# A decoder block: cross-attention in two passes with keys on partitions, and expert weights spread by DMA and multiplied in by GpSimd

## The chip, the cores and the metric

The kernel runs on one core of a Trainium2 chip. The core has five engines that run side by side and wait for each other by semaphores: TensorE (PE, matrix multiplications into PSUM), VectorE (DVE), ScalarE (ACT), GpSimd (POOL) and SyncE (SP, which here only issues DMAs). The metric is the time of one execution on the device in microseconds; the lower the better.

## The reference: what is computed

A block of a decoder over 128 sequences of 64 tokens with 128 features each. Three stages follow each other, each with a layer norm ahead and a residual behind:

```
x = x + attention(norm(x))          # 16 heads of 64, through 8 pooled "agent" queries per head
x = x + cross_attention(norm(x), ctx, ctx)   # 16 heads of 8, causal mask, softmax over 64 keys
x = x + ffn(norm(x))                # 16 experts of 64, each token takes 2; and one shared layer

scores  = Q K^T / sqrt(8) + causal                 # cross-attention, per sequence and head
out     = (softmax(scores) V) Wo^T
combine = one_hot(top 2 of 16 by a gate) * gate weight      # ffn, 16 numbers a token
h       = silu(x We1 + be1) * (x We3 + be3)                 # all experts for all tokens
y       = sum over e of combine[e] * (h[e] We2[e] + be2[e])
```

## The kernel before

The 128 sequences are taken in 8 groups of 16, 1024 tokens each. Each engine has its own program, written out by hand, and all five follow the same plan, `both(e, g)`: the feed-forward of group e is interleaved with the two attentions of group e + 1 = g. Nothing reorders it later: an engine that waits holds all that stands behind it in its own program. `both(None, 0)` opens, seven calls of `both(e, e + 1)` follow, `both(7, None)` closes.

The feed-forward goes in 18 units k = 0 to 17: two chunks of 512 tokens, in each one shared layer and then eight pairs of experts, with the hidden features of a pair on 128 partitions and tokens along the free dimension. A unit is `up(e, k)`, two groups of three fp32r matmuls over 512 tokens (rows L491 to L493) into the banks H1 and H3; SiLU of H1 by ACT into `sil` (L874); for a pair a bf16 matmul `weight`, named C, that spreads the combine weights over the partitions (L500); two passes of DVE, `hidden_3` (L1166) and `weighted` (L1173), which make `hT`; and `down_to(e, k)`, four fp32 matmuls that add hT times w2 to Y (L510). `unit(e, k)` issues `up(k)`, C, and `down_to(k - 1)`. The C matmul needs the combine weights with experts on partitions: DVE's `gate` makes them, split into three bf16 parts, and PE transposes them.

The cross-attention goes in four rounds u of four sequences. `scores` puts queries on partitions and heads and keys along the free dimension, in four banks S (L598 the mask, L606 the scores, on tiles of 32 rows and 64 columns). DVE takes the maximum over keys (`maxima`, L1219, L1221) and subtracts it (L1222), ACT takes the exponential into `pr` (L930, L935), DVE sums and inverts (`inverses`, L1233, L1235), POOL normalises 14 of the 16 blocks (L426) and DVE two. Then PE transposes the probabilities (`turn`, L624), ACT copies them (`PT_moved`), and PE multiplies with the values (`values`, L635) and projects (`project`, L648). `add_x` (L1239) adds the residual; a layer norm (`norm`, POOL's power, `apply`, L1080) gives xn3, the input of the feed-forward.

The first attention begins with `moments`, 8 blocks M_0 to M_7 of four fp32 matmuls (L674) on pooled sums (L1286), then `scores_1` (L541) and `scores_2` (L552), `soften` on DVE (subtracting maxima, L1187 to L1193), exponentials on ACT, `normalise_2` on DVE (three passes, L1200 to L1202), transposes of the probabilities p1T and p2T, `pool_tokens` (L581) and three more blocks. In the feed-forward of the same call these stand between the units; `gate_shift` and `gate` (L1088 to L1144) are DVE's part of the choice of experts, from the gate matmul (L720) on.

Where the rows name a tile as `PXUT`, `KQ` or `M`, it is the buffer in which the tile of that moment lies; several share one.

Of the kernel before, what the change touches and what calls it, by code (L numbers as in the profile page):

```python
# [6 lines left out]
def decoder_block(nc, x, ctx_in, Wqkv, Wo_a, bo, Wq, Wk, Wv, Wo_x, gate_w, gate_b,  # L7
# [16 lines left out]
    B, S, D = x.shape  # L24
    P = 128
# [12 lines left out]
    BY_DVE = (XQ * UX - 4, XQ * UX - 3)  # L38
    BY_POOL = [k for k in range(XQ * UX) if k not in BY_DVE]
# [3 lines left out]
    CHUNKS = TOK // CH  # L43
    EPS = 1e-5
# [12 lines left out]
    att = ["ctxT_0", "ctxT_1", "V_0", "V_1", "V_2", "xnT1_0", "xnT1_1", "V_3", "KT_0"]  # L57
    att += [f"M_{n}" for n in range(8)]
    att += ["s1_0", "s1_1", "s2_0", "KT_1", "s1_2", "s1_3", "s2_1"]
    att += ["p1T_0", "p2T_0", "PX_0", "PX_1", "p1T_1", "p2T_1", "PX_2", "PX_3"]  # L60
    att += [f"UT_{n}" for n in range(4)] + [f"U_{n}" for n in range(4)] + ["Ya_0", "Ya_1"]
    att += ["xnT2_0", "xnT2_1", "QT_0", "QT_1"] + [f"S_{n}" for n in range(XQ * UX)]
# [4 lines left out]
             "h1": (["xnT3_0"] + [f"H1_{k}" for k in range(UNITS)], 1),  # L67
             "h3": (["xnT3_1"] + [f"H3_{k}" for k in range(UNITS)], 1),
             "c": (["gate", "combS"] + [f"C_{k}" for k in PAIRED if k < EP + 1] + ["combT_0", "combT_1"]
                   + [f"C_{k}" for k in PAIRED if k > EP], 1),  # L70
             "y": (["Y_0", "Y_1"], 1),

             "pt": ([f"PT_{n}" for n in range(2 * T)], 2),
             "ol": ([f"OL_{u}" for u in range(UX)], 1),
# [7 lines left out]
    with ExitStack() as ctx:  # L82
# [9 lines left out]
        Kx, Qx = KQ[:, 0:4, :], KQ[:, 4, :]  # L92
# [14 lines left out]
        woM = sb("woM", [P, 2, 2, D])  # L107
# [13 lines left out]
        identb = sb("identb", [P, P], bf16)  # L121
        maskb = sb("maskb", [P, 2, HALF, S], bf16)
        pick = sb("pick", [P, 2, S], bf16)
        planes = sb("planes", [P, 4, 4])
        plane = sb("plane", [P, 4])
        onehot3 = sb("onehot3", [P, E], bf16)
        spread = sb("spread", [P, EP, 2, EI], bf16)
# [11 lines left out]
        xnT3 = sb("xnT3", [P, TOK])  # L139
# [27 lines left out]
        Vb = sb("Vb", [P, T, XH // 2, 2, 2 * XC])  # L167
        mx = sb("mx", [P, XQ, HALF])
        lx = sb("lx", [P, 2, XQ, HALF])
        rx = sb("rx", [P, 2, XQ, HALF])  # L170

        PR = 3 * XQ
        pr_a = PXUT[:].rearrange("p a b h -> p (a b h)").rearrange("p (k h s) -> p k h s", k=2 * XQ, s=S)
# [16 lines left out]
        comb = sb("comb", [P, T, 2 * E])  # L190
        combs = sb("combs", [P, T, P], bf16)
        combT = sb("combT", [P, TOK])
        combsT = sb("combsT", [P, TOK], bf16)
        sil = sb("sil", [P, 2, CH])
        hT = sb("hT", [P, 2, CH])

# [1177 lines left out]
```

## Time and profile before

| what | us |
|---|---|
| median of 3 runs (1148.31 to 1152.15) | 1151.69 |
| the profiled execution: span from first to last instruction | 1150.6 |
| PE busy in it | 975.8 (85%) |
| DVE busy | 788.8 (69%) |
| ACT busy | 577.3 (50%) |
| POOL busy | 227.7 (20%) |

The share of busy time says little by itself: two stretches alternate eight times, one filled by PE, and one in which the engines wait for each other in turn. The chain of waits tells them apart, as does the busy time by window. In rows of the timeline, a group of instructions stands with its start, its length, the engine, the line, what it writes from what, and how many records it has; fp32 matmuls leave two records each. In brackets stands the idle time before it and who ended it. The granted clock of PE is given as a share of 2.4 GHz, so 0.50 is 1.2 GHz.

### The profile page before, as it was taken

Reading aid. Unit: us, or ns where it says so; the run is one execution under the profiler, and the core shown is the slowest. Engines: PE = TensorE matmul, PEld = TensorE weight load, DVE = VectorE, ACT = ScalarE, POOL = GpSimd, SP = SyncE. Lnnn points to the kernel's source line nnn. Section 1 sums busy time; section 2 is a strip of 40 time slices with the busy share of each in tenths; the row PEclk is TensorE's granted clock in tenths of the full one; section 3 lists DMA queues with packets and bytes.
Section 4 is the critical chain, followed back from the end, with each engine's and each line's share of the span. In section 5 each row is a group of like instructions: output and inputs, shape, how many; then the busy total and the mean of one; then the engine's idle time right before and its main releaser. Section 6 shows DMA issues by size and latency. Waiting matters only on the chain.

```text
span 1150.6 us, 22137 instructions
## 1 busy us (share of the span) xinstructions
PE 975.8 (85%) x9069; PEld 767.2 (67%) x9069; DVE 788.8 (69%) x1841; ACT 577.3 (50%) x1148; POOL 227.7 (20%) x220
## 2 busy tenths in 40 slices
PE   6656899969998799978999699987999689987687
PEld 5553688737785587846886487855787477864566
DVE  3256866687866967678667878678666867669444
ACT  4434755367534665357553565346652575445322
POOL 6001410035000520024100440014200341004100
PEclk9886999979998899979999799989999799997789
DMA  5300010000100010000100010000100000000000
GB/s 146 80 1 1 2 38 1 11 10 2 38 10 10 2 38 1 11 10 2 37 11 1 11 31 8 10 11 2 38 1 10 11 2 1 10 11 1 1 1 19
DMA packets 28902, 18.36 MB, mean 16 GB/s; under 512 B 7649, under 2 KB 27394, under 8 KB 28802
## 3 DMA queue, kind: packets, MB, share of 16 engines
q1 hardware_dynamic: 26914, 12.48, 4.2%
q0 software_dynamic: 1280, 4.20, 1.2%
q8 instruction: 72, 1.18, 0.4%
q10 hardware_dynamic: 608, 0.27, 0.1%
q14 instruction: 28, 0.23, 0.1%
HBM read 12.62 MB, written 4.19 MB: 15 GB/s over the span
## 4 chain that ended last, share of the span: by engine, by line
PE 62%; DVE 21%; ACT 10%; POOL 3%; issue 3%; SPq 1%; DMA 0%; DVEq 0%; POOLq 0%
PE banks L510 7%; PE banks L674 5%; PE banks L491 5%; PE banks L493 5%; PE banks L492 5%; PE banks L606 4%; PE banks L624 4%; ACT M L867 3%; PE banks L648 3%; DVE PXUT L1222 3%; DVE mx L1221 3%; PE banks L769 3%; PE banks L541 2%; DVE sil L1166 2%; PE banks L598 2%
## 5 line engine op out<-in xcount | busy, mean ns | idle before, releaser
L874 ACT ACTIVATE sil<-banks,b 128x512 f32<-128x512 f32 x144 | 99.5, 691 | 199.6 <-PE banks L493 197.2
L867 ACT COPY M<-banks 128x512 f32<-128x512 f32 x208 | 122.9, 609 | 90.3 <-PE banks L624 70.2
L1166 DVE SCALAR_TENSOR_TENSOR sil<-banks,b,sil 128x512 f32<-128x512 f32 x128 | 95.8, 749 | 93.6 <-ACT sil L874 91.8
L510 PEld LDWEIGHTS banks<-w,hT 128*128 128x128 f32 x1152 | 151.5, 194 | 12.5 <-issue 7.2
L510 PE MATMUL banks<-w,hT 128*128 128x128 f32 x1152 | 154.5, 277 | 1.4 <-DVE hT L1173 1.4
L389 POOL DMA_DIRECT2D out_x<-xn x16 | 12.9, 809 | 534.3 <-DVE xn L1179 534.3
L426 POOL TENSOR_TENSOR PXUT<-PXUT,rx 128x512 f32<-128x512 f32 x80 | 87.2, 1117 | 101.7 <-DVE rx L1235 101.7
L1173 DVE TENSOR_TENSOR hT<-sil,banks 128x512 f32<-128x512 f32 x128 | 87.9, 687 | 25.1 <-PE banks L500 21.3
L624 PE MATMUL banks<-ident,PXUT 128*128 128x128 f32 x384 | 61.9, 301 | 31.7 <-ACT M L867 28.2
L598 PE MATMUL banks<-maskb,pick 32*64 32x512 bf16 x512 | 46.4, 506 | 46.6 <-ACT PXUT L930 28.2
L674 PEld LDWEIGHTS banks<-pooled,A 128*128 128x128 f32 x512 | 66.1, 207 | 19.9 <-DVE pooled L1286 18.6
L624 PEld LDWEIGHTS banks<-ident,PXUT 128*128 128x128 f32 x384 | 44.1, 150 | 52.6 <-ACT M L867 40.0
L674 PE MATMUL banks<-pooled,A 128*128 128x128 f32 x512 | 68.9, 293 | 12.0 <-DVE pooled L1286 12.0
L491 PE MATMUL banks<-xnT3l,w1h 128*128 128x512 f32 x144 | 75.1, 522 | 0.3 <-ACT sil L874 0.3
L491 PE MATMUL banks<-xnT3l,w3h 128*128 128x512 f32 x144 | 61.4, 427 | 11.1 <-DVE sil L1166 10.3
L1221 DVE TENSOR_REDUCE mx<-banks 128x8 f32<-128x512 f32 x96 | 65.3, 681 | 0.0
L867 ACT COPY PXUT<-banks 128x512 f32<-128x512 f32 x64 | 36.0, 588 | 54.6 <-PE banks L581 30.7
L606 PE MATMUL banks<-KQ 32*64 32x256 f32 x1024 | 60.9, 547 | 0.0
L493 PE MATMUL banks<-xnT3h,w1h 128*128 128x512 f32 x144 | 59.3, 412 | 0.0
L493 PE MATMUL banks<-xnT3h,w3h 128*128 128x512 f32 x144 | 59.2, 411 | 0.0
L1233 DVE TENSOR_REDUCE lx<-PXUT 128x8 f32<-128x512 f32 x96 | 59.2, 658 | 0.0
L492 PE MATMUL banks<-xnT3h,w1l 128*128 128x512 f32 x144 | 59.2, 411 | 0.0
(199 smaller groups left out, 2067.2 us busy)
## 6 DMA issues: line engine op xcount, KB each, us to landing
xin<-in_x SPq DMA_DIRECT2D x8, 512.0 KB, 4.1
cin<-in_ctx SPq DMA_DIRECT2D x8, 512.0 KB, 5.3
out_x<-xn POOLq DMA_DIRECT2D x16, 256.0 KB, 2.8
KQ<-in_L_attn_Wqkv SPq DMA_DIRECT2D x3, 512.0 KB, 5.3
KQ<-in_L_ffn_We SPq DMA_DIRECT2D x2, 512.0 KB, 4.6
KQ<-in_L_attn_Wo SPq DMA_DIRECT2D x1, 512.0 KB, 8.0
w<-in_L_ffn_We SPq DMA_DIRECT2D x1, 512.0 KB
woM<-xwT SPq DMA_DIRECT2D x16, 8.0 KB, 1.8
```

What stands on the lines that cost most here:

```text
L491: mm(ps(name)[:], wh[:, 2 * p:2 * p + 2, :], xl, start=True, stop=False)
L492: mm(ps(name)[:], wl[:, 2 * p:2 * p + 2, :], xh, start=False, stop=False)
L493: mm(ps(name)[:], wh[:, 2 * p:2 * p + 2, :], xh, start=False, stop=True).then_inc(fulled(name), 1)
L510: mm(ps(name)[:, P * t:P * t + P], hT[:, k % 2, P * t:P * t + P], w2[:, pair[k], :], start=(n == 0 and t == 0), stop=False, skip_group_che ...
L606: last = mm(ps(name)[64 * r:64 * r + 64, 256 * t:256 * t + 256], Qx[rr, S * b:S * b + S], Kx[rr, :, S * b:S * b + S], start=False, stop=Tr ...
L624: last = turn_over(ps(name)[:, P * j:P * j + P], src[:, P * j:P * j + P], ident[:])
L674: last = mm(ps(f"M_{n}")[:, P * k:P * k + P], A[:, 4 * (n % 4) + k, :], pooled[:], start=True, stop=True)
L867: cp(dst, ps(name)[:] if src is None else src).then_inc(ready, 1)
L874: nc.scalar.activation(sil[:, k % 2, :], ps(f"H1_{k}")[:], ACT.Silu, bias=b1[:, pair[k]:pair[k] + 1]).then_inc(sil_ready, 1)
L1166: V.scalar_tensor_tensor(sil[:, k % 2, :], ps(f"H3_{k}")[:], b3[:, p:p + 1], sil[:, k % 2, :], ALU.add, ALU.mult).then_inc(hid_ready, 1)
L1173: V.tensor_tensor(hT[:, k % 2, :], sil[:, k % 2, :], ps(f"C_{k}")[:], ALU.mult).then_inc(hT_ready, 1)
L1221: link(V.tensor_reduce(mx[:, q], sv, AX, ALU.max), g)
```

## The change

The cross-attention is done in two passes. The first keeps the scores with queries on partitions, but only their maxima are taken. These, one per query and head, are split in three bf16 parts and transposed into `shiftT` (`split_shifts`, `turn_shifts`). In the second pass `scores_T` computes the scores again with keys on partitions, with the mask and the negated maximum added by a bf16 matmul (`pickT` and `shiftT`), so that ACT takes the exponential straight from PSUM and the probabilities need no transpose. The values carry a column of ones (`Vx`), so that `values` gives the sums too, and `normalise_O` divides the 8 columns of a head by the ninth. `turn_O`, a copy and `project` follow.

The combine weights are transposed in fp32, written to DRAM (`comb_d`) and read back by two DMAs a unit, each spreading one expert's row over 64 partitions, into a ring of four (`cw`). POOL multiplies them into `sil` (`weight` of POOL), and `hidden` is one pass of DVE. `down_to` runs two units behind `up` (`LAG`), H3 has two banks.

The order changes too. The rounds of first-pass scores stand between units 13 to 16, and the transposes and moments of the next group stand in the second pass. The core of the diff:

```
-    att = ["ctxT_0", "ctxT_1", "V_0", "V_1", "V_2", "xnT1_0", "xnT1_1", "V_3", "KT_0"]
-    att += [f"M_{n}" for n in range(8)]
+    front = ["ctxT_0", "ctxT_1", "xnT1_0", "xnT1_1"] + [f"M_{n}" for n in range(8)]
...
+             "h1": (["xnT3_0", "H1_0", "H1_1", "combT_0", "combT_1"] + [f"H1_{k}" for k in range(2, UNITS)], 1),
+             "h3": (["xnT3_1"] + [f"H3_{k}" for k in range(UNITS)], 2),
+             "f": (front, 2),
...
+            def weights_spread(e):
+
+                sp.wait_ge(combT_ready, 2 * e + 2)
+                sp.dma_start(comb_d.ap(), combT[0:E, :]).then_inc(comb_stored, 16)
+                sp.wait_ge(comb_stored, 16 * e + 16)
+                for n, k in enumerate(PAIRED):
+                    use = len(PAIRED) * e + n
+                    c, p = k // (EP + 1), pair[k]
+                    if use >= CW:
+                        sp.wait_ge(weighted, use - CW + 1)
+                    for a in range(2):
+                        row = comb_d.ap()[2 * p + a, CH * c:CH * c + CH]
+                        sp.dma_start(cw[EI * a:EI * a + EI, use % CW, :],
+                                     row.partition_broadcast(EI)).then_inc(cw_loaded[use % CW], 16)
...
+            def weight(e, k):
+
+                if e is None or k not in PAIRED:
+                    return
+                use = len(PAIRED) * e + PAIRED.index(k)
+                pool.wait_ge(cw_loaded[use % CW], 32 * (use // CW) + 32)
+                pool.wait_ge(sil_ready, UNITS * e + k + 1)
+                s = sil[:, k % (LAG + 1), :]
+                nc.gpsimd.tensor_tensor(s, s, cw[:, use % CW, :], ALU.mult).then_inc(weighted, 1)
...
+            def scores_T(g, u):
+
+                names = [f"ST_{XQ * u + q}" for q in range(XQ)]
+                if u == 0:
+                    pe.wait_ge(mT_ready, g + 1)
+                for q, name in enumerate(names):
                     wait_free(pe, g, name)
...
+                    for j in range(2):
+                        mm(ps(name)[:, 256 * j:256 * j + 256], pickT[:, 2 * q + j, :, :],
+                           shiftT[:, 256 * u:256 * u + 256], start=(j == 0), stop=False, skip_group_check=True)
+                for j in range(2):
+                    for k in range(4):
+                        b = 4 * u + k
+                        for q, name in enumerate(names):
+                            rr = slice(32 * q, 32 * q + 32)
+                            c0 = 256 * j + S * k
+                            last = mm(ps(name)[:, c0:c0 + S], Kx[rr, j, b, :],
+                                      Qx[rr, S * b:S * b + S], start=False, stop=True, skip_group_check=True,
+                                      tile_position=(32 * q, 0))
...
+                pe.wait_ge(ex_ready, XS * g + XQ * u + XQ)
+                for t in range(2):
+                    for j in range(XH // 2):
+                        for r in range(2):
+                            k = 2 * t + r
+                            c0, w = 256 * (j % 2) + S * k, 2 * (XC + 1)
+                            o0 = w * (XH // 2) * t + w * j
+                            last = mm(ps(name)[64 * r:64 * r + 64, o0:o0 + w],
+                                      PT[:, XQ * (u % 2) + j // 2, c0:c0 + S], Vx[:, 4 * u + k, j, :],
+                                      start=True, stop=True)
...
+                wait_full(act, g, f"ST_{k}")
+                nc.scalar.activation(PT[:, k % (2 * XQ), :], ps(f"ST_{k}")[:], ACT.Exp).then_inc(ex_ready, 1)
...
+                wait_full(dve, e, f"H3_{k}")
+                if k in PAIRED:
+                    dve.wait_ge(weighted, len(PAIRED) * e + PAIRED.index(k) + 1)
...
+                p, slot = pair[k], k % (LAG + 1)
+                V.scalar_tensor_tensor(hT[:, slot, :], ps(f"H3_{k}")[:], b3[:, p:p + 1], sil[:, slot, :],
+                                       ALU.add, ALU.mult).then_inc(hT_ready, 1)
```

Three places where the programs' order changes. The first is PE's program from the last values of a group to the gate matmul of its feed-forward, before (L635 are the values, L648 the projection, L674 the moments, L720 the gate):

```order
L635 MATMUL banks<-M,Vb 32x128 x16
L660 MATMUL banks<-xwT,ctxT 64x64 x8
L648 MATMUL banks<-woM,KQ 64x128 x8
L469 MATMUL banks<-ident,xn 128x128 x8
L660 MATMUL banks<-xwT,ctxT 64x64 x8
L666 MATMUL banks<-ctxT,xwT 128x512
L674 MATMUL banks<-pooled,A 128x128 x16
L469 MATMUL banks<-ident,xn 128x128 x8
L674 MATMUL banks<-pooled,A 128x128 x4
L720 MATMUL banks<-gwT,xnT 128x16 x8
```

And after the change (L658 are the values, L667 `turn_O`, L676 the projection, L546 and L557 `scores_1` and `scores_2`, L745 the gate):

```order
L658 MATMUL banks<-Vx,PXUT 64x18 x32
L667 MATMUL banks<-ident,KQ 128x128 x2
L676 MATMUL banks<-xwT,KQ 128x128 x2
L688 MATMUL banks<-xwT,ctxT 64x64 x32
L488 MATMUL banks<-ident,xn 128x128 x8
L546 MATMUL banks<-xnT,M 128x128 x8
L557 MATMUL banks<-M,xnT 64x128 x8
L745 MATMUL banks<-gwT,KQ 128x16 x8
```

The moments and the first transposes (L469 with 8 matmuls ahead of L660) no longer stand between the projection and the gate; the values of the next group's keys (L688) do, and the first score blocks stand ahead of the gate.

The second is DVE's program where the combine weights are done, after the change (L1145 is the last pass of `gate`, L1186 to L1188 are `normalise_2`, L1158 is `hidden`):

```order
L1145 TENSOR_TENSOR comb<-gate 128x8x16
L1186 TENSOR_REDUCE l<-PXUT 128x64
L1187 RECIPROCAL r<-l 128x64
L1188 TENSOR_TENSOR PXUT<-PXUT,r 128x512
L1158 SCALAR_TENSOR_TENSOR hT<-banks,b,sil 128x512
L1186 TENSOR_REDUCE l<-PXUT 128x64
L1187 RECIPROCAL r<-l 128x64
L1188 TENSOR_TENSOR PXUT<-PXUT,r 128x512
L1158 SCALAR_TENSOR_TENSOR hT<-banks,b,sil 128x512
```

The L1158 in the middle is `hidden` of unit 1, the first that needs combine weights. Before, the two `normalise_2` stood after the hidden passes of units 4 and 5.

The third is PE's program in the second pass, after the change, from the first round's transposed scores (L633 mask and shift, L641 scores) to the third round's moments (L702):

```order
L633 MATMUL banks<-shiftT,pickT 128x256 x8
L641 MATMUL banks<-KQ 128x64 x32
L488 MATMUL banks<-ident,xn 128x128 x8
L658 MATMUL banks<-Vx,PXUT 64x18 x32
L633 MATMUL banks<-shiftT,pickT 128x256 x8
L641 MATMUL banks<-KQ 128x64 x32
L667 MATMUL banks<-ident,KQ 128x128 x2
L702 MATMUL banks<-pooled,A 128x128 x8
L676 MATMUL banks<-xwT,KQ 128x128 x2
L658 MATMUL banks<-Vx,PXUT 64x18 x32
```

Between the scores and the values of a round stands work of the next group, and the projection of the round before.

## Rows read from the trace of the kernel before

**Rows 1.** Chain of waits in order of time: start us, us, what.

```profile
43.02 1.14 DVE pooled L1286
...
142.29 1.14 DVE pooled L1286
...
940.58 1.14 DVE pooled L1286
```

**Rows 2.** Busy by window: window, us, PE, PEld, DVE, ACT, POOL (instructions), clock, DMA.

```profile
365.00:375.00 10.00, 5.37 (x73) 2.27 (x81) 7.87 (x14) 4.79 (x13) 0.79 (x1) 0.60 0.09 26
```

**Rows 3.** Groups by line: what, how many, busy us, mean ns, idle before.

```profile
L426 POOL TENSOR_TENSOR PXUT<-PXUT,rx 128x512 f32<-128x512 f32 x80 | 87.2, 1117 | 101.7 <-DVE rx L1235 101.7
```

**Rows 4.** Timeline of PE, feed-forward of group 1 to first scores: start us, us.

```profile
303.60 0.58 PE L491 MATMUL banks<-xnT3l,w1h 128*128 128x512 f32 x1
...
341.21 0.48 PE L491 MATMUL banks<-xnT3l,w1h 128*128 128x512 f32 x1
...
342.69 0.39 PE L500 MATMUL banks<-combsT,spread 128*128 128x512 bf16 x1
...
343.74 0.48 PE L491 MATMUL banks<-xnT3l,w1h 128*128 128x512 f32 x1
...
360.71 1.04 PE L606 MATMUL banks<-KQ 32*64 32x256 f32 x32
```

**Rows 5.** Timeline of PE, other small matmuls (weights rows*columns, then moving shape).

```profile
30.71 1.62 PE L660 MATMUL banks<-xwT,ctxT 128*64 128x64 f32 x48 [0.78 <-ACT ctxT L867]
...
276.52 3.84 PE L674 MATMUL banks<-pooled,A 128*128 128x128 f32 x32 [0.40 <-DVE pooled L1286]
...
282.50 1.96 PE L720 MATMUL banks<-gwT,xnT 128*128 128x16 f32 x16 [0.38 <-ACT xnT L867]
...
316.38 1.16 PE L581 MATMUL banks<-p1T,xn 64*128 64x128 f32 x16
```

**Rows 6.** Timeline of DVE: `apply` of xn3, and `add_x` one period on.

```profile
277.09 2.14 DVE L1080 TENSOR_SCALAR xn<-xe,norm_e 128x128 f32<-128x128 f32 x8 [0.62 <-POOL norm_e L397]
...
406.58 0.42 DVE L1239 TENSOR_TENSOR xe<-xr,banks 128x256 f32<-128x256 f32 x1 [0.24 <-PE banks L648]
```

**Rows 7.** Timeline of DVE: from `gate_shift` to the last pass of `gate`.

```profile
284.50 0.29 DVE L1088 TENSOR_REDUCE g<-banks 128x8 f32<-128x128 f32 x1 [5.27 <-PE banks L720]
...
293.56 0.75 DVE L1166 SCALAR_TENSOR_TENSOR sil<-banks,b,sil 128x512 f32<-128x512 f32 x1 [0.94 <-ACT sil L874]
...
297.22 0.29 DVE L1144 TENSOR_TENSOR combs<-gate,combs 128x128 bf16<-128x128 f32 x1
```

**Rows 8.** Timeline of DVE: `soften` and what follows it, `normalise_2` and what follows it.

```profile
297.43 0.42 DVE L1187 TENSOR_REDUCE m<-banks 128x4 f32<-128x256 f32 x1
...
300.34 0.68 DVE L1173 TENSOR_TENSOR hT<-sil,banks 128x512 f32<-128x512 f32 x1
...
314.89 0.68 DVE L1200 TENSOR_REDUCE l<-PXUT 128x64 f32<-128x512 f32 x1
...
316.80 0.74 DVE L1166 SCALAR_TENSOR_TENSOR sil<-banks,b,sil 128x512 f32<-128x512 f32 x1
```

**Rows 9.** Timeline of ACT: a copy of transposed combine weights, and its wait for PE.

```profile
330.35 0.57 ACT L867 COPY combT<-banks 32x512 f32<-32x512 f32 x1 [0.45 <-PE banks L477]
```

**Rows 10.** DMA issues: what, queue, how many, KB each, median us to landing.

```profile
xin<-in_x SPq DMA_DIRECT2D x8, 512.0 KB, 4.1
...
woM<-xwT SPq DMA_DIRECT2D x16, 8.0 KB, 1.8
```

**Rows 11.** Busy by window, columns as in rows 2: where the clock fell and rose.

```profile
366.00:367.00 1.00, 0.45 (x16) 0.35 (x24) 1.00 (x2) 0.47 (x1) 0.00 (x0) 0.96 0.00 0
...
377.00:378.00 1.00, 1.00 (x7) 0.60 (x5) 0.97 (x3) 0.53 (x2) 1.00 (x2) 0.92 0.00 0
```

**Rows 12.** Timeline of POOL at the start, and of PE at the last xn3.

```profile
18.54 0.66 POOL L380 TENSOR_SCALAR_AFFINE_SELECT maskb<-maskb 32x512 bf16<-32x512 bf16 x1
...
1078.29 1.97 PE L469 MATMUL banks<-ident,xn 128*128 128x128 f32 x8 [5.88 <-DVE xn L1080]
```

More of the change, by code:

```diff
@@ L37, in decoder_block @@
     UX = T // 2
-    BY_DVE = (XQ * UX - 4, XQ * UX - 3)
-    BY_POOL = [k for k in range(XQ * UX) if k not in BY_DVE]
+    XS = XQ * UX
     E, EG, EI = 16, 4, 64
@@ L268, in wait_free @@
             ring, k, use, _, at = place[name]
+            if not use and ring in ("o", "yx") and not g:
+                return
             if use:
@@ L962, in both @@
+            def both(e, g):
+                nxt = g + 1 if g is not None and g + 1 < GROUPS else None
+                if e is None:
+                    ctx_moved(g)
+                    xn_moved(g)
+                    for n in range(8):
+                        M_moved(g, n)
+                if g is not None:
                     for n in range(4):
-                        M_moved(g, n)
+                        V_moved(g, n)
                 if e is not None:
@@ new lines, in both @@
+                if g is not None:
+                    apply("a", xr, xn, rstd_ready, 2 * g + 2, xn_ready, lambda: hidden(e, 8))
+                else:
+                    hidden(e, 8)
+                for k in range(9, 11):
+                    hidden(e, k)
+                result(e, 0)
+                hidden(e, 11)
+                hidden(e, 12)
+                for u in range(UX):
+                    if g is not None:
+                        maxima(g, u)
+                    hidden(e, 13 + u)
@@ new lines, in both @@
+                if g is not None:
+                    split_shifts(g)
+                hidden(e, 17)
+                result(e, 1)
+                if g is None:
+                    return
+                if nxt is not None:
+                    dve.wait_ge(x_loaded, 16 * nxt + 16)
+                    norm(nxt, "a", xin, var_ready)
+                    apply("a", xin, xn, rstd_ready, 2 * nxt + 1, xn_ready)
+                for u in range(UX):
+                    normalise_O(g, u)
+                    if u == 0 and nxt is not None:
+                        dve.wait_ge(xnT_ready, 4 * nxt + 2)
+                        V.tensor_reduce(pooled[:], xnT[:, 0:TOK].rearrange("p (k s) -> p k s", s=S // POOL), AX,
+                                        ALU.add).then_inc(pooled_ready, 1)
+                    if u:
+                        add_x(g, u - 1)
+                        if u < UX - 1:
+                            stats_e(g, u - 1)
```

719 lines of the change are left out of this document (298 added, 421 removed).

## The prediction

> **What bounds the kernel now.** I read the busy times first (TensorE, PE, is busy 85% of the span, no other engine above 69%), then the chain of waits in order of time, then one period of the timeline engine by engine. The chain repeats: the pooled sums of group 1 start at 142.29 and those of group 7 at 940.58 [rows 1], so a group takes (940.58 - 142.29) / 6 = 133.05 us. In the feed-forward stretch PE is the bound: a unit of the hidden layer is `up` (six matmuls, 341.21 to 342.69), the combine-weight matmul C and `down` (to 343.74), and the next starts at once [rows 4]. In the cross-attention PE waits: from 365 to 375 it is busy 5.37 of 10 us at 0.60 of its clock while VectorE (DVE) is busy 7.87 [rows 2]. So two things can gain: PE's own units, and this second stretch.
>
> **The change part by part.** All times below run along one new period, from the moment T at which the normalised rows xn3 are ready to the next T. Prices are at the full granted clock first; the clock is a term of its own. A PE row's time runs some 0.1 us into the next row's; that is taken off.
>
> *Passes taken off.* Sixteen hT passes, twelve subtractions, sixteen sums and the normalising of the probabilities leave DVE and GpSimd (POOL). That is worth only what PE waited for them. On PE a unit loses C: 1.05 us for C and `down` together, of which C is a 512-column matmul like one of the six in `up`, 1.48 / 6 = 0.25; a unit goes from 2.53 to 2.29 [rows 4], 18 x 0.24 = 4.3 us per group. POOL's 16 new multiplications take the place of 14 old ones of the same shape, 1.12 us each [rows 3]; at one per 2.29 us unit, with `down` now two units behind, they are hidden.
>
> *1. From T to the combine weights: 18.7 us.* PE does the xn3 transposes (8 single passes, each half of a 276.52 matmul: 0.9), two score blocks (8 matmuls like those of the 276.52 row, 1.8, and half-width ones, 0.5) and the gate (1.81, the 282.50 row) [rows 5]: gate full at T+5.1. DVE is in soften(0) until then, does gate_shift (0.65) and then soften(1), which stands ahead of the gate now and takes 300.34 - 297.43 = 2.9 [rows 8]; its last input comes at T+7.4, so it ends at T+9.0. The chain in the old order ran from 284.50 to 297.51 = 13.0 [rows 7]. Off go gate_shift and its exponential (two passes of 0.29 and one of 0.3 on ScalarE, 1.0), the hidden pass that moves with its wait (0.94 + 0.75), and the splitting (four passes like the 297.22 row, 1.05); 9.3 remain, and 0.4 of waiting for the first SiLU, which queues behind soften(1)'s exp. T+18.7. PE has 12.2 us of work in that time (0.9 + 1.8 + 0.5 + 1.8 + 1.8 + 0.5, two `up` and the keys, 2.0); the moments that filled it are gone to the other end of the period. 6.4 us idle.
>
> *2. From there to the transpose p2T_1: 11.9 us.* The weights are transposed twice through one bank, 0.65 + 0.57 + 0.65 + 0.57 with the copies [rows 9] = 2.5; written to DRAM (2.3, between 1.8 for 8 KB and 4.1 for 512 KB [rows 10]); read back spread over 64 partitions, twice (2.4 by the same rows, and 0.45 for the second issue); multiplied by POOL (1.1) and DVE (0.75). Behind DVE's hidden(1), which waits for all this, is queued normalise_2(1) (316.80 - 314.89 = 1.9 [rows 8]), and PE's p2T_1 waits for that, with all units from 3 on behind it. Five semaphore hops, 0.5. PE has 6.6 us of work here, so 5.3 idle. Bounds: 10.8 with both transfers at 1.8, 15.5 with both at 4.1.
>
> *3. From p2T_1 to the end of the feed-forward: 57.6 us.* PE-bound as before. From unit 3 to the end of the first scores it took 303.60 to 361.75 = 58.15 [rows 4]. Off: 14 C (3.4), three of four transposes of the probabilities (1.4), one pooling block (1.1), two weight transposes (0.9), old waits (1.8). On: two `down` (1.6), the bias matmuls (0.9), three score rounds (3 x 1.45), new waits (1.2: each score round waits for four maxima). Each score round now hides behind a unit, which is the change's real gain: DVE needs 3.4 of the 3.8 us.
>
> *4. The second pass: 39.2 us.* Per round, eight bf16 matmuls of 256 columns (half of C, 0.12 each: 1.0), 32 of 64 columns on 32-row tiles, and 32 value matmuls of 18 columns. The trace has none of these two. In records of a weight load with its pass (two per fp32 matmul), the nearest rows: 32 records on 32-row tiles in 1.04 us, 33 ns [rows 4]; 16 on 64-row tiles in 1.16 (68 ns with the next start), 48 with 64-column weights in 1.62 (34 ns), 16 of 16 columns on the whole array in 1.81 (113 ns) [rows 5]. I take 33 ns x 64 = 2.1 for the transposed scores (1.0 if it goes by columns, 4.4 by the 68 ns) and 34 ns x 64 = 2.2 for the values (1.1; 3.6, half of 113 ns for half the weight columns). Four rounds of 5.3 = 21.2. Between scores and values PE waits for four exponentials (0.6 each, like the copy of [rows 9], a copy among them and hops: 3.0), which moments partly fill: round 0 waits for xn of the next group, ready 7.3 after the pass starts (3.3); round 1 3.0; rounds 2 and 3 hold three moments of 0.92 [rows 5] over two banks, whose third waits for a copy behind the exponentials (4.9 each). 16.1, and 1.85 for the shifts' transposes and copy: 39.2.
>
> The Trainium skill, "TensorE: Matmul & The Clock Gate", section "LDWEIGHTS (loading the stationary operand)", says that a load's time follows the weight's columns and not its depth. By its figure 128 columns are 107 ns (an estimate from that page of the Trainium skill), and a round's 64 loads one after the other 6.8 us instead of 2.1. The 16-record row on 64-row tiles [rows 5] speaks against that for tiles, with 68 ns for such a load.
>
> *5. From the last values to T: 8.7 us.* normalise_O (0.85), transpose, copy and projection (1.6), then the old chain from add_x to xn3: 406.58 less a period is 273.53, to 277.09 + 2.14 = 279.23: 5.7 [rows 6], plus 0.5 for two more statistics. PE has 3.0 of filler (values of the next group); 4.2 idle at a stretch.
>
> Sum: 18.7 + 11.9 + 57.6 + 39.2 + 8.7 = 136.1 us, against 133.05. The old waits of the cross-attention come back as three waits of DVE and DMA chains that no PE work covers.
>
> *6. The clock: +7 us per period.* In the old period the clock fell to 0.5 (1.2 GHz) at 366.9 after some 4 us in which PE did little, and rose at 377.2 [rows 11]: 10 us, which cost some 5. The measured 133.05 holds that already. The old tail shows PE idle 5.88 us behind the chain of part 5 [rows 12]. The new period has four such places: the idle of 5 (1.5), of 1 (0.5, hidden by 2), of 2 (2, on units that bound) and the sparse first rounds of 4 (3). These are estimates from that stretch; bounds 0 and 14.
>
> *7. Head, last group, tail.* First T before: 1078.29 - 7 x 133.05 = 146.9. GpSimd's five new masks of 64 x 1024 (at least 0.66 each [rows 12], 1.2 by size) and larger clears bring the constants 6.3 later, but the pooled sums no longer wait for the expert weights (43.02 [rows 1], now 36.7). The key copies on ScalarE give 5 of these back, 2.3 remain. From the first scores to T it was 279.23 + 133.05 - 360.71 = 51.6; now four rounds of 4.1 without units, the splitting (17.7), 38.4 and 8.7 = 64.8, and clock 3. Head +13.9. The last group has no moments: -5.5. Tail: 14 units x 0.24 less the longer start, -1.4.
>
> Total: 1150.6 + 13.9 + 7 x (136.1 + 7 - 133.05 = 10.05) - 5.5 - 1.4 = 1228; the profiled span is 1 us below the median, so **1229**.
>
> **The rivals.** *Full clock.* As above with 6 at nothing: 1150.6 + 10.9 + 7 x 3.05 - 6.9 = 1176. For it: PE's longest hole is 5.3. Against: it fell after less at 366.9 [rows 11]. *The other side: small matmuls go by their columns and the clock holds.* Then 4 is 4 x 2.2 = 8.8 shorter, the period 127.3: 1150.6 + 2.1 - 7 x 5.75 - 6.9 = 1106. It decides from a period of 133, that is, if 4 loses more than the 3 us by which the sum is over. *Loads one after the other*: by the 113 ns row a round is 7.2 instead of 2.1, 32 rounds x 5.1 = +163: 1392; the 68 ns row speaks against it. It is where the rule of the Trainium skill cited above would lead. *Transfers that set the pace* instead of only the start: a ring of four units (9.2 us) covers 4.1 + 0.9, so only 2 grows, by 8 x 3.6 at most: 1258, inside the range.
>
> **How the numbers follow.** Forecast with the clock's term 0.56, full clock 0.18, loads in series 0.04: slower 0.78. Columns and clock 0.18 faster; 0.04 lands within 0.3%, about what a measurement here can tell from no change. The prices' ends are -70 and +118, the clock's -50 and +50, seldom together: 1140 to 1300 leaves out most of the faster case (0.14) and the serial loads (0.04).
>
> **What would show it.** Right: PE idle some 6 us before the weight transposes and 5 before p2T_1, the latter released by DVE behind hidden(1); a period near 143; granted clock 0.5 after these. Wrong: value and score records far off 34 and 33 ns; PE idle under 2 us at either place; DVE or GpSimd as releaser in most units.

## The result, and the profile after

The changed kernel takes 1258.38 us (median of 4 runs, 1257.78 to 1260.06) against 1150.47 for the kernel before: a ratio of 1.094, 95% interval 1.092 to 1.096. Forecast were 1229 and slower; the range 1140 to 1300 holds the time. The medians and ratios below leave out one run as slow, 1200.47 us of the three edits together.

The chain of waits of the changed kernel, in order of time (start us, length us, what), shows the places T at which xn3 is ready, eight in all; it answers to [rows 1] and the `apply` of [rows 6]:

```profile
156.18 2.15 DVE xn L1088 x8
...
301.07 2.15 DVE xn L1088 x8
447.49 2.15 DVE xn L1088 x8
593.79 2.15 DVE xn L1088 x8
...
1034.17 2.15 DVE xn L1088 x8
1183.05 2.15 DVE xn L1088 x8
```

So the first T is at 158.3, the periods are 144.9, then five of 146.3 to 147.2, and the last 148.9. The period from T = 303.2 to 449.6 is the one that the parts below are read from. Its timeline of PE, from the first two `up` to unit 4 (L496 turns the combine weights over, L574 is p2T_1, L510 begins an `up`):

```profile
319.12 0.39 PE L512 MATMUL banks<-xnT3h,w3h 128*128 128x512 f32 x1
324.37 1.04 PE L496 MATMUL banks<-ident,comb 128*32 128x128 f32 x4 [4.86 <-DVE comb L1145]
...
333.03 0.66 PE L567 MATMUL banks<-ident,e 128*128 128x128 f32 x4
337.51 1.09 PE L574 MATMUL banks<-ident,PXUT 128*128 128x128 f32 x4 [3.83 <-DVE PXUT L1188]
338.25 0.78 PE L510 MATMUL banks<-xnT3l,w1h 128*128 128x512 f32 x1
...
343.03 0.50 PE L510 MATMUL banks<-xnT3l,w1h 128*128 128x512 f32 x1
```

PE's two longest waits here are 4.86 us before the weights' transposes and 3.83 before p2T_1; behind the second the `up` of unit 3 takes 0.78 where that of unit 4 takes 0.50. The granted clock by window (window, us, PE, PEld, DVE, ACT, POOL busy, clock, DMA share, GB/s) says why:

```profile
322.00:324.00 2.00, 0.00 (x0) 0.00 (x0) 1.78 (x7) 2.00 (x4) 0.00 (x0) 0.97 0.00 0
324.00:326.00 2.00, 1.04 (x4) 0.43 (x4) 1.91 (x4) 0.73 (x2) 0.00 (x0) 0.50 0.00 0
...
328.00:330.00 2.00, 2.00 (x8) 1.71 (x7) 0.00 (x0) 1.16 (x2) 0.00 (x0) 0.50 0.24 41
...
338.00:340.00 2.00, 2.00 (x7) 1.71 (x6) 1.71 (x5) 0.67 (x2) 0.00 (x0) 0.50 0.26 94
```

The second pass, same timeline (L633 the pick, L641 transposed scores, L658 values, L488 the next group's transposes):

```profile
400.73 2.01 PE L641 MATMUL banks<-KQ 32*128 32x64 f32 x64
405.24 1.49 PE L488 MATMUL banks<-ident,xn 128*128 128x128 f32 x8 [2.50 <-DVE xn L1088]
406.66 3.61 PE L658 MATMUL banks<-Vx,PXUT 128*64 128x18 f32 x64
410.20 1.89 PE L633 MATMUL banks<-shiftT,pickT 128*128 128x256 bf16 x8
412.02 3.69 PE L641 MATMUL banks<-KQ 32*128 32x64 f32 x64
...
420.03 2.05 PE L658 MATMUL banks<-Vx,PXUT 128*64 128x18 f32 x64
422.01 1.05 PE L633 MATMUL banks<-shiftT,pickT 128*128 128x256 bf16 x8
422.99 2.01 PE L641 MATMUL banks<-KQ 32*128 32x64 f32 x64
...
431.40 1.05 PE L633 MATMUL banks<-shiftT,pickT 128*128 128x256 bf16 x8
...
438.82 2.05 PE L658 MATMUL banks<-Vx,PXUT 128*64 128x18 f32 x64
```

PE waits 2.50 us for xn of the next group; from then to about 419 its clock is 0.50, and the same 64 records take 3.6 us instead of 2.0:

```profile
406.00:408.00 2.00, 2.00 (x30) 1.67 (x28) 0.00 (x0) 1.10 (x2) 0.00 (x0) 0.50 0.00 0
...
418.00:420.00 2.00, 2.00 (x13) 1.91 (x11) 0.00 (x0) 0.96 (x3) 0.00 (x0) 0.64 0.00 0
```

A round at full clock takes 9.39 (422.01 to 431.40). Spans and mean granted clock, of the kernel before and then of the changed one:

```profile
core 0: 1150.6 us, clock 0.921
```

```profile
core 0: 1256.3 us, clock 0.880
```

At two levels, 1.0 and 0.5, that is 2 x 0.079 x 1150.6 = 182 us at half clock before, and 2 x 0.120 x 1256.3 = 301 after: 120 us more, worth up to 60 of the 106 us wherever PE is the bound. Whole periods, columns as above: one before, then the one above and the last group's after the change:

```profile
279.23:412.28 133.05, 117.75 (x1126) 92.61 (x1125) 97.12 (x230) 70.72 (x143) 26.32 (x22) 0.94 0.05 13
```

```profile
303.22:449.64 146.42, 126.22 (x1420) 108.25 (x1420) 70.51 (x183) 54.59 (x96) 31.65 (x24) 0.90 0.14 41
...
1036.32:1185.20 148.88, 122.33 (x1276) 102.81 (x1276) 65.21 (x159) 44.97 (x76) 30.00 (x23) 0.80 0.11 33
```

Of the 13.4 us by which a period grew, PE is busy for 8.5 and waits for 4.9. By the same sum these periods hold some 16, 29 and 60 us at half clock, and the last one of the kernel before (944.40 to 1078.25, granted clock 0.91) 24, so the last group alone brings some 36 of the 120.

### The profile page after: what moved, and what is told of

The parts are those of the page before. It is cut to its first block, busy times and chain, and to the rows that moved or that the text cites. A ratio compares the mean times of both kernels' runs of the same rounds, so it can differ in the third digit from the quotient of the medians.

```text
span 1256.3 us, 26341 instructions
## 1 busy us (share of the span) xinstructions
PE 1041.8 (83%) x11437; PEld 885.6 (70%) x11437; DVE 574.6 (46%) x1473; ACT 449.3 (36%) x782; POOL 276.7 (22%) x239
## 4 chain that ended last, share of the span: by engine, by line
PE 58%; DVE 16%; issue 10%; ACT 8%; POOL 7%; POOLq 0%; DVEq 0%; ACTq 0%
PE banks L521 6%; PE banks L658 6%; PE banks L641 5%; PE banks L510 4%; PE banks L702 4%; DVE xn L1088 4%; PE banks L511 3%; PE banks L512 3%; PE banks L546 3%; ACT PXUT L946 3%; PE banks L633 3%; PE banks L488 2%; POOL sil L403 2%; PE banks L611 2%; PE banks L777 2%
## 5 line engine op out<-in xcount | busy, mean ns | idle before, releaser
L403 POOL TENSOR_TENSOR sil<-sil,M 128x512 f32<-128x512 f32 x128 | 162.8, 1273 | 462.8 <-ACT sil L890 301.2
L1158 DVE SCALAR_TENSOR_TENSOR hT<-banks,b,sil 128x512 f32<-128x512 f32 x144 | 107.2, 748 | 239.6 <-POOL sil L403 234.7
L946 ACT ACTIVATE PXUT<-banks 128x512 f32<-128x512 f32 x128 | 69.4, 609 | 156.3 <-PE banks L641 156.3
L702 PE MATMUL banks<-pooled,A 128*128 128x128 f32 x512 | 76.9, 312 | 12.2 <-ACT M L883 10.3
L702 PEld LDWEIGHTS banks<-pooled,A 128*128 128x128 f32 x512 | 72.4, 225 | 15.3 <-ACT M L883 13.0
L658 PEld LDWEIGHTS banks<-Vx,PXUT 128*64 128x64 f32 x2048 | 76.6, 163 | 8.2 <-issue 5.9
L658 PE MATMUL banks<-Vx,PXUT 128*64 128x18 f32 x2048 | 79.8, 229 | 3.0 <-ACT PXUT L946 3.0
L510 PE MATMUL banks<-xnT3l,w1h 128*128 128x512 f32 x144 | 76.3, 530 | 7.0 <-ACT sil L890 6.4
L641 PEld LDWEIGHTS banks<-KQ 32*128 32x128 f32 x2048 | 74.7, 226 | 8.5 <-issue 8.5
L641 PE MATMUL banks<-KQ 32*128 32x64 f32 x2048 | 79.5, 314 | 0.0
L488 PE MATMUL banks<-ident,xn 128*128 128x128 f32 x192 | 32.2, 322 | 54.8 <-DVE xn L1088 54.8
L510 PE MATMUL banks<-xnT3l,w3h 128*128 128x512 f32 x144 | 60.9, 423 | 6.9 <-DVE hT L1158 6.9
L488 PEld LDWEIGHTS banks<-ident,xn 128*128 128x128 f32 x192 | 25.6, 163 | 57.5 <-DVE xn L1088 36.1
L883 ACT COPY M<-banks 128x512 f32<-128x512 f32 x80 | 46.2, 608 | 55.7 <-PE banks L574 31.2
```

Source lines behind the costliest of these rows:

```text
L403: nc.gpsimd.tensor_tensor(s, s, cw[:, use % CW, :], ALU.mult).then_inc(weighted, 1)
L488: last = turn_over(ps(name)[:, P * t:P * t + P], src[:, 4 * n + t, :], ident[:])
L510: mm(ps(name)[:], wh[:, 2 * p:2 * p + 2, :], xl, start=True, stop=False)
L641: last = mm(ps(name)[:, c0:c0 + S], Kx[rr, j, b, :], Qx[rr, S * b:S * b + S], start=False, stop=True, skip_group_check=True, tile_position ...
L658: last = mm(ps(name)[64 * r:64 * r + 64, o0:o0 + w], PT[:, XQ * (u % 2) + j // 2, c0:c0 + S], Vx[:, 4 * u + k, j, :], start=True, stop=True)
L702: last = mm(ps(f"M_{n}")[:, P * k:P * k + P], A[:, 4 * (n % 4) + k, :], pooled[:], start=True, stop=True)
```

## The experiments

All medians below stand against 1258.38 for the changed kernel and about 1150 for the kernel before, measured beside each run; ratios are to the kernel before, with their 95% interval.

### VectorE's order at hidden(1)

```diff
-hidden(e, 1)
 normalise_2(g, 1)
+hidden(e, 1)
 hidden(e, 2)
```

> VectorE normalises the probabilities of the second half (normalise_2(1)) before hidden(1) instead of behind it; nothing else differs from the changed kernel (1258). Theory A, that TensorE's wait of 3.8 us before the transpose p2T_1, and the low clock behind it (four of the six matmuls of unit 3 at 0.43 instead of 0.23 us), come only from the place of normalise_2(1) behind an instruction that waits for the DMA round trip: p2T_1 follows p1T_1 at once, up(3) waits some 0.5 us for hidden(1) to free its bank, a period loses 4 to 5 us in seven groups: 1223 to 1230. Theory B, that the round trip of the weights itself bounds the feed-forward: the wait only moves from p2T_1 to up(3) or down(1), less than 1 us a period: 1251 to 1258.

Measured: 1233.14 (1.071, 1.067 to 1.075), 25 us less. p2T_1 now follows p1T_1 at once; what is left of that is a wait of 1.50 us in unit 3, for the bank that hidden(1) frees:

```profile
329.69 0.66 PE L567 MATMUL banks<-ident,e 128*128 128x128 f32 x4
330.19 0.60 PE L574 MATMUL banks<-ident,PXUT 128*128 128x128 f32 x4
...
332.99 0.50 PE L510 MATMUL banks<-xnT3l,w3h 128*128 128x512 f32 x1 [1.50 <-DVE hT L1158]
```

Theory A by the wait, 3 us above its range.

### The round trip without its delay

```diff
 def weights_spread(e):
-    wait combT(e); write comb_d; wait for it
+    if 0 < e < 7: wait until the first score blocks are read
     for n, k in enumerate(PAIRED):
+        if n == (CW if e else 0):
+            wait combT(e); write comb_d[e % 2]; wait for it
-        load row of comb_d
+        load row of comb_d[max(e - 1, 0) % 2]
```

> From the second group on, the feed-forward multiplies with the combine weights of the group before, which lie in DRAM already, so the first four loads start once the first score blocks are read, some 15 us before this group's weights exist, and hidden(1) waits for no round trip. It leaves the route by DRAM as it is and takes away its delay alone. Theory A, that the delay of the round trip costs the wait before p2T_1 and the clock behind it: 5 us in six groups and 3 us in the last, 1220 to 1230. If the order on VectorE is all that matters, this comes out within 5 us of the run that only swaps two instructions there. Theory B, that the pace of the 32 loads or of GpSimd's multiplications bounds the units: less than 10 us in all, 1248 to 1258.

Measured: 1237.22 (1.076, 1.074 to 1.079), 7 us above theory A's range and within 5 us of the swap. The wait before p2T_1 is gone, and each period from the second on is within 0.3 us of the swap's; the 4 us between the two runs are the first period, whose group still waits for its own weights (148.0 against 142.1), less 2 us ahead of it. So the round trip costs through what is queued behind the instruction that waits for it, and neither GpSimd nor the 32 loads set the pace of the units. That its length as such costs nothing is not shown: GpSimd's first product now falls into VectorE's `gate`, where one pass takes 1.28 us instead of 0.29, and PE waits 5.85 us instead of 4.86 before the weights' transposes, which may hide some 1 us a period.

### The next group's rows normalised earlier

```diff
 hidden(e, 11)
+norm(nxt, "a", xin, var_ready)
 hidden(e, 12)
 for u in range(UX):
     maxima(g, u)
     hidden(e, 13 + u)
+    apply of xn, tiles 2u and 2u + 1
 ...
 result(e, 1)
-norm(nxt, "a", xin, var_ready)
-apply("a", xin, xn, rstd_ready, 2 * nxt + 1, xn_ready)
```

> The next group's statistics are taken after hidden(11) and its rows normalised in four parts behind the maxima, instead of all between result(1) and the second pass; GpSimd's rstd stands after its weight 12. All else as in the changed kernel (1258). In the changed kernel TensorE waits 2.5 us for these rows in the first round of the second pass and then works some 13 us at half clock (405.9 to 419). Theory A, that this wait is what lowers the clock there: a period loses 2.5 us and about half of 13, 8 to 9 us in seven groups, 1195 to 1205, and the granted clock stays 1.0 through the second pass. Theory B, that the sparse small matmuls of the second pass lower the clock whatever happens to this wait: a loss of 1 to 2.5 us a period, 1240 to 1251.

Measured: 1223.26 (1.064, 1.061 to 1.067), 35 us less, between the two theories. The clock did what A says, 1.00 over the whole second pass (398.31 to 433.63); timeline and windows of this run:

```profile
402.99 1.09 PE L488 MATMUL banks<-ident,xn 128*128 128x128 f32 x8
405.29 2.05 PE L658 MATMUL banks<-Vx,PXUT 128*64 128x18 f32 x64 [1.20 <-ACT PXUT L946]
407.27 1.05 PE L633 MATMUL banks<-shiftT,pickT 128*128 128x256 bf16 x8
```

```profile
406.00:408.00 2.00, 2.00 (x53) 1.90 (x51) 0.59 (x2) 0.11 (x1) 0.00 (x0) 1.00 0.03 8
408.00:410.00 2.00, 2.00 (x67) 1.79 (x65) 1.31 (x2) 0.00 (x0) 0.00 (x0) 1.00 0.00 0
```

The second pass from the shifts' transposes (398.31) to the last values (433.63) takes 35.3 us instead of 42.9. Part of that is given back: a new wait of 1.20 for the exponentials, `hidden(17)` 0.4 later behind the moved passes, 4.30 instead of 2.80 us of waiting before the next xn3, and a head 4 us longer. Per middle period 6.5 us remain.

### More work in the last group

```diff
 for u in range(UX):
     scores_T(g, u)
+    if nxt is None: transposes (u == 0) or moments (u > 0) of old data, into banks nobody reads
```

> In the last group TensorE repeats, in the second pass, the eight transposes and the 32 moment matmuls that the other groups do there for their successor, on old data and into banks that nobody reads; 40 instructions more, nothing else differs from the changed kernel (1258). My prediction had the last group 5.5 us shorter for lack of them. Theory A, that the last group's second pass is slow because without them the clock falls after round 0 and stays at half to the gate (rounds of 11.7 us against 9.4): the rounds come down to some 9.4 and the run gets faster by 5 to 9 us, 1249 to 1253, though work is added. Theory B, that the extra work (some 8 us at full clock) lies on the path: 1262 to 1268.

Measured: 1249.59 (1.087, 1.084 to 1.089), 8.8 us less with 40 instructions more: theory A. The windows of the last second pass, the changed kernel first, then this run:

```profile
1144.00:1152.00 8.00, 7.11 (x108) 6.39 (x106) 0.00 (x0) 2.34 (x5) 0.00 (x0) 0.50 0.01 2
1152.00:1160.00 8.00, 7.11 (x83) 5.79 (x82) 1.59 (x5) 2.25 (x5) 0.00 (x0) 0.50 0.00 0
```

```profile
1144.00:1152.00 8.00, 8.00 (x184) 7.50 (x182) 1.60 (x5) 2.34 (x5) 0.00 (x0) 1.00 0.01 2
1152.00:1160.00 8.00, 8.00 (x162) 7.50 (x160) 1.60 (x5) 2.34 (x5) 0.00 (x0) 1.00 0.01 2
```

PE was busy 7.1 of 8 us there at half clock, and the clock didn't rise. It had fallen behind a wait of 2.23 us ahead of the first values (1138.18); with the eight transposes in that place 1.20 us of waiting are left, and with the moments behind them the clock was 1.00 to the end of the pass. Which of the two fillings holds it was not parted. The last period is now 137.1 us instead of 148.9, about the 137.6 of the forecast.

### The three together, and with two waits filled

> The changed kernel with three edits together: normalise_2(1) ahead of hidden(1), the next group's rows normalised ahead of the second pass, and the last group's second pass filled with repeated transposes and moments. If each takes away a wait of its own, the gains of 25, 35 and 9 us add up: 1185 to 1195, still slower than the kernel before. If they are the same slack counted twice (TensorE's clock recovers only once a period): 1205 to 1220.

Measured: 1193.25 (1.035, 1.028 to 1.042; 1182 to 1197). 65 of the 69 us add up. Within this one run the same code has periods of 134.45 and 140.16; rows of its chain, and windows at the same place of the first and of the second of these periods (102 us behind each start):

```profile
293.30 1.68 POOL norm_e L418
...
427.75 1.67 POOL norm_e L418
...
567.91 1.67 POOL norm_e L418
```

```profile
395.30:401.30 6.00, 6.00 (x133) 5.63 (x131) 1.91 (x3) 1.84 (x6) 0.00 (x0) 1.00 0.01 3
...
529.80:535.80 6.00, 5.83 (x116) 5.18 (x116) 1.90 (x3) 1.00 (x3) 0.00 (x0) 0.71 0.01 3
535.80:541.80 6.00, 6.00 (x50) 5.87 (x46) 0.00 (x0) 3.46 (x7) 0.00 (x0) 0.50 0.02 3
```

Of the 5.7 us between them 4.8 lie in the second pass, between its first values and the round after them, and are the clock; 1.0 lies ahead of it. Both passes wait the same 1.20 us before these values (394.56 and 529.97), so why the clock fell in the one and not in the other is open. All seven periods sort by it: four second passes have a mean clock of 1.00, in periods of 133.4 to 135.0, and three have 0.85, in periods of 140.1 to 140.3. Where the clock holds, the two-pass period is thus within 2 us of the 133.05 of the kernel before.

```diff
+ten matmuls of 512 columns
 pe.wait_ge(xn3_ready, e + 1)
 ...
+18 matmuls of 512 columns
 pe.wait_ge(comb_ready, e + 1)
```

> The three edits, and TensorE fills two of the waits that remain with matmuls whose results nobody reads: ten of 512 columns ahead of the transposes of xn3, and 18 ahead of the transposes of the combine weights (4.2 us, for a wait of 4.9). Theory A, that it is the waiting that lowers the clock for the work that follows it (3 us at half clock behind T, 6 behind the weights): the granted clock stays 1.0 there and a group gains 2 to 4 us, 16 to 32 us below the three edits alone. Theory B, that DVE's gate chain and the round trip set the pace there and TensorE's clock does not matter: within 6 us of the three edits alone.

Measured: 1180.61 (1.024, 1.018 to 1.031; 1170 to 1186), 13 us less, between the two theories and nearer to A's 16; its granted clock is 1.0 where the run before it has 0.60 (the window 316 to 322 of both). Part of the gain is waited away at once: before the bank that `hidden(1)` frees, in unit 3, PE waits 2.27 us instead of 0.79.

### Each half of the change alone

```diff
 # kernel before, with the new feed-forward
-C_k = spread x combsT on PE; hT = (H3 + b3) * sil * C on DVE, two passes; one unit of delay
+weights by comb_d and GpSimd; hT = (H3 + b3) * sil, one pass; two units of delay
+agent attention's softmax, normalise_2 and turn_probs(0) right behind the gate
```

> The feed-forward half of the change alone: the kernel before with its own cross-attention, but the combine weights go by DRAM to partitions, GpSimd multiplies them in, the third product has two banks and the second product comes two units later. Transposes, softmax and normalising of the agent attention stand behind the gate so that they cover the round trip. Theory A, by my sums: 18 times 0.24 us less on TensorE per period against 3 to 6 us of the round trip that stays uncovered, so close to the kernel before, 1135 to 1165. Theory B, that the route of the weights by DMA and GpSimd is what makes the changed kernel slow: most of the 105 us shows up here, 1200 or more.

Measured: 1180.23 (1.024, 1.020 to 1.029), above A's range and below B's. PE's two longest waits in the feed-forward are 2.11 us before p2T_0 and this one at unit 15, which the new order brought (first VectorE, then PE):

```profile
349.06 4.59 DVE L1081 TENSOR_SCALAR xn<-xr,norm_a 128x128 f32<-128x128 f32 x4 [1.10 <-POOL norm_a L431]
```

```profile
354.37 0.51 PE L512 MATMUL banks<-xnT3l,w3h 128*128 128x512 f32 x1 [3.41 <-DVE hT L1151]
```

```diff
 # changed kernel, with the old feed-forward
-weights by comb_d and GpSimd, one pass of VectorE, two units of delay
+C_k = spread x combsT on PE, two passes of VectorE, one unit of delay
```

> The cross-attention half of the change alone: the changed kernel with the combine weights multiplied in as before (split in three, one TensorE matmul a unit, two VectorE passes, one unit of delay), no DRAM, no GpSimd. Theory A: of the period of 146.4 us some 8 of the 13.3 between weights and p2T_1 go, and 18 times 0.24 us on TensorE come back, 142 to 143 a period: 1222 to 1235, so the second pass and the waits around it are most of the loss. Theory B, that the two-pass attention costs nothing by itself: 1150 to 1165.

Measured: 1293.91 (1.124, 1.122 to 1.127): a miss, for both theories. The period is 150.3 against 146.4. By its timeline the weights come 1.6 us later and p2T_1 follows 3.5 us sooner behind them, but the stretch from p2T_1 to the end of the feed-forward is 65.2 instead of 60.5 and the second pass 1.0 longer. So in the two-pass layout the new feed-forward is a gain, 36 us. Which of its pieces gives it (no C, one VectorE pass less between the maxima, the second unit of delay) was not taken apart.

### GpSimd beside VectorE

```diff
-tensor_tensor(s, s, cw[:, use % CW, :], ALU.mult)
+tensor_tensor(s[:, 0:8], s[:, 0:8], cw[:, use % CW, 0:8], ALU.mult)
```

> GpSimd multiplies only the first 8 of the 512 columns of each weight tile (the rest of the hidden units stays unweighted); waits, loads and order are those of the changed kernel (1258). In its trace VectorE's normalising passes are longer wherever GpSimd works at the same time: four passes of `apply` for xr in 2.06 us at 362.94, while eight without GpSimd take 2.14 (403.04), and a pass of split_shifts 1.40 instead of 0.29 at 393.36. Theory A, that VectorE's pass is held up by GpSimd's: `apply` for xr comes back to 0.27 a tile, the split pass to 0.3, and with 1.2 us less on the round trip a period loses 2 to 3.5 us: 1234 to 1244. Theory B, that the passes are slow for another reason (xr's place in memory, the clock of VectorE): they stay at 0.5 a tile, and only the 1.2 us on the round trip is gained, 1248 to 1256.

Measured: 1235.88 (1.076, 1.071 to 1.080), theory A. Groups by line (count, busy us, mean ns, idle before), the changed kernel and then this run:

```profile
L1088 DVE TENSOR_SCALAR xn<-xr,norm_a 128x128 f32<-128x128 f32 x64 | 31.0, 545 | 9.5 <-POOL norm_a L411 9.5
L1211 DVE TENSOR_TENSOR md<-mx,mparts 128x128 f32<-128x128 f32 x8 | 9.0, 1121 | 0.3
```

```profile
L1088 DVE TENSOR_SCALAR xn<-xr,norm_a 128x128 f32<-128x128 f32 x64 | 17.7, 340 | 9.5 <-POOL norm_a L411 9.5
L1211 DVE TENSOR_TENSOR md<-mx,mparts 128x128 f32<-128x128 f32 x8 | 2.3, 292 | 0.3
L403 POOL TENSOR_TENSOR sil<-sil,M 128x8 f32<-128x8 f32 x128 | 25.8, 201 | 566.4 <-ACT sil L890 372.5 <-DMA M<-comb_d 193.8
```

### The feed-forward half, rearranged

```diff
-UT, U, Ya behind the units 8, 9, 10
+UT, U, Ya behind the units 6, 7, 8
-apply of xr: four tiles, hidden(13), four tiles
+hidden(11), two tiles, hidden(12), two tiles, hidden(13), two tiles, hidden(14), two tiles
-normalise_2(1), hidden(1)
+hidden(1), normalise_2(1)
```

> The run with the feed-forward half alone (1180), with the agent attention's products two units earlier and VectorE's normalising of xr in four parts behind the units 11 to 14, and hidden(1) ahead of normalise_2(1). In that run TensorE waited 3.4 us for VectorE at unit 15 (the first four passes of `apply` took 4.59 us beside GpSimd) and worked some 5 us at half clock behind it. Theory A, that these were the loss and not the weights' route: 4 to 6 us less in seven periods, 1138 to 1152, so level with the kernel before. Theory B, that the route by DMA and GpSimd costs more than TensorE's matmul saves wherever it stands: 1170 to 1180.

Measured: 1147.97 over 10 runs (0.998, 0.9965 to 0.9999): theory A. In this order the half comes out level with the kernel before, so what C saved is given back; PE still waits 2.11 us before p2T_0, and its clock behind that is 0.50 (303 to 306). `hidden(1)` stands here ahead of normalise_2(1), the other way round than in the swap above; what that alone does here was not measured.

> The same, and TensorE fills the waits of the round trip with matmuls that nobody reads, 16 of 512 columns a group (4 ahead of the weights' transposes, 3 ahead of p1T_0, 9 ahead of p2T_0; 3.7 us at full clock). In the run with the feed-forward half alone these waits are 0.9, 0.8 and 2.1 us, and the 8 us behind them run at half clock. Theory A, that waiting lowers the clock of the units that follow: the clock stays 1.0 there, 2 to 4 us less a group than without the filling, 16 to 30 us less in all, below the kernel before. Theory B, that the filling only delays what is on the path: 0 to 12 us more.

The first four of its 16 fillers go into the bank in which the second product of unit 0 already stands, so that product is lost. Measured: 1136.19 over 4 runs (1134 to 1144; 0.988, 0.984 to 0.992), 12 us less, below what theory A asks for.

> The rearranged feed-forward half (1148) with the 16 idle matmuls a group once more, the first four now written into the bank that the weights' transposes use next, so that nothing of the output is touched: the version that the other runs point to. Theory A, that the filling holds TensorE's clock behind the round trip: as the run before it, 1132 to 1142, below both kernels. Theory B, that its gain came from the overwritten first product: no gain, 1146 to 1152.

Measured: 1147.15 over 12 runs (1144 to 1149; 0.9966, 0.9952 to 0.9979), theory B by the time; it is 0.3% below the kernel before, the fastest that computes everything, and no more than level. The clock behind the round trip is 1.00 in both filled runs, and yet the period of this one is that of the unfilled: 133.1 (from the `apply` at 337.18 to the one at 470.32) against 133.0. In the cross-attention that follows, the clock then stays low longer: from 360 to 372, in windows of 3 us, 0.55, 0.50, 0.50 and 0.74, against 0.75, 0.68, 0.89 and 0.50 in the unfilled run. VectorE is busy 15.4 and 15.5 of the 18 us behind 360, so it fits that what PE wins ahead of this stretch is waited away in it; no run tests that. In unit 3, too, PE waits 1.73 us for `hidden(1)` where the unfilled run has 0.47. Why the 4 runs of the first of the two filled ones were faster is open. The two differ in the lost product and in where the first fillers stand: in the second they wait 0.80 us for the SiLU of unit 2 to free their bank. The profiled execution of the first was the slowest of its four, with a span within 1 us of the second's, so the traces can't tell.

## Why the prediction held, part by part

From 303.2 to 449.6, forecast with its share of the clock's term, and measured:

| part | forecast | measured |
|---|---|---|
| 1. T to the weights | 18.7 + 1.5 | 21.1 |
| 2. to p2T_1 | 11.9 + 0.5 | 13.2 |
| 3. to the end of the feed-forward | 57.6 + 2 | 60.5 |
| 4. second pass | 39.2 + 3 | 42.9 |
| 5. to T | 8.7 | 8.8 |
| sum (of unrounded parts) | 143.1 | 146.4 |

**Parts 1 and 2** named the right waits: 4.86 us before the weights' transposes (forecast 6.4) and 3.83 before p2T_1 (5.3), the latter released by VectorE behind hidden(1). That the queue behind hidden(1) makes the second wait is shown by the swap, which leaves the transfer as it is and takes the wait away. The chain itself, by the DMA queue and GpSimd:

```profile
327.74 0.33 SPq L318 DMA_DIRECT2D comb_d<-combT  x1
```

```profile
333.33 1.27 POOL L403 TENSOR_TENSOR sil<-sil,M 128x512 f32<-128x512 f32 x1 [22.90 <-DMA M<-comb_d]
```

From the write's issue to the product it is 5.6 us, forecast 2.3 + 2.85; the product takes 1.27, forecast 1.1. The table load of 1.28 us ahead of the first SiLU (ScalarE, 315.81) was not in part 1.

**Part 3.** A unit is 2.30 us (359.61 to 361.91), as forecast, and score rounds hide behind units. What failed is that GpSimd was taken to be free of cost once it keeps up: VectorE's `apply` for xr takes 545 ns a tile beside it (343 before), and a pass of the splitting 1.12 us. Shortening GpSimd's instruction gave 22 us, part of it the 1.1 us on the round trip in each group; the rest I put down to the passes, without having parted the two.

**Part 4** came out right by luck. The prices of the records were good: 64 score records take 1.94 us from start to start (30 ns each, forecast 33) and 64 value records 1.98 (31, forecast 34), so they don't go by their columns (1.0 and 1.1), and that rival is out with its steady clock. The rival of loads one after the other, for which the Trainium skill is cited above, is out: a round's 64 score loads have 128 columns and went by in 1.94 us, not 6.8. But at full clock the pass is 35.3 us, as the run with the early rows shows (one wait of 1.20 in place of 2.50), not 39.2: the waits for exponentials and banks were priced too high. And the clock's share was priced too low: 3 us, where 13.6 us of this period's second pass run at half clock, which is up to 6.8. The two nearly cancel.

**Part 6, the clock**, was the right term: with early rows, with the filled last group and with two waits filled the clock is 1.00 where it was 0.50 to 0.60, and the time falls; the rival of a full clock is out. Its size was right in places. By part, some 4, 6, 4, 14 and 3 us of this period are at half clock, worth at most half of that: the 1.5 and 2 us forecast for parts 1 and 3 are about what was found, the 3 of part 4 are less than half. One consequence was missed altogether: **the last group**. I took 5.5 us off for the moments that it doesn't have; it is some 2 us longer than the five before it instead, 11.3 from the forecast. The work taken away was what kept the clock up: with it put back the period is 137.1.

**The sum.** The last group gives 11.3 of the 29 us missing, the six other periods 19.4, head and tail -2.3, the time outside the span 1.

**Where the expected gain went.** C is gone and the score rounds hide, but in the old layout the weights' route is level with C at best (1148 against 1150), and the changed kernel adds waits of PE on chains through VectorE, ScalarE and DMA, behind which its clock is low. With the three edits 42 us are still lost (1193), with two more waits filled 30. The trace of the three edits says where: of the 41 us by which its span is longer than before, 16 lie ahead of the first T (162.6 against 146.9) and 27 in the seven periods, most of that in the three whose second pass runs at 0.85; the tail gives 1 back. The head wasn't taken apart.

## What to carry to other kernels

An instruction that waits for a transfer should stand behind everything on its in-order engine that doesn't need the transfer: here two swapped passes were worth as much as no delay at all. A gap on TensorE can be paid twice, once as waiting and once as half clock for the work behind it; before removing filler from a sparse stretch, ask what holds the clock there. Work moved to GpSimd has a price on VectorE too, even when GpSimd itself is never waited for.

## What the runs showed of the hardware

A busy TensorE is no sign of a full clock: from 1144 to 1168 of the changed kernel it was busy 7.1 to 8 of each 8 us at 0.50 throughout; with transposes and moments between the same instructions it was at 1.00. And the same code, behind the same wait of 1.20 us, ran at 1.00 in one second pass and fell to 0.50 in another of the same execution (the three edits).

VectorE's fp32 pass with per-partition scalars over 128 columns takes 0.27 us a tile alone and up to 1.1 beside GpSimd (four in 4.59 us at 349.06 of the run with the feed-forward alone); a pass with two operands in SBUF 0.29 and 1.40, about GpSimd's 1.27. The pass `hidden`, with one operand in PSUM, isn't touched: 107.2 us for 144 in the changed kernel, 107.7 with GpSimd shortened. The Trainium skill, "SBUF — State Buffer", section "Who interferes with whom", has this: the two engines share one pair of ports, held for a whole instruction, and a VectorE instruction takes part if it runs in a two-port mode or reads two operands from SBUF. The traces agree for the pass with two operands in SBUF and for the one with an operand in PSUM; for the first pass they agree if it runs in a two-port mode, which no run here shows. It would have added a term to part 3.
